# A sparse-graph kernel on one core: a new order of tile visits, a fifth sum bank, and VectorE's half of the split two visits later

## What is computed

```python
for _ in range(3):
    v = mlp(A @ u, uv_W1, uv_b1, uv_W2, uv_b2, uv_W3, uv_b3)
    u = mlp(A @ v, vu_W1, vu_b1, vu_W2, vu_b2, vu_W3, vu_b3)
x = layernorm(x + v)
out = layernorm(x + A @ (x @ weight))
```

## Time and profile before

| | |
|---|---|
| median of three executions | 1225.14 us |
| the profiled execution | 1227.23 us |
| its span, first to last instruction | 1225.5 us |
| mean granted TensorE clock | 0.984 |
| PE busy | 1173.3 us (96%), 5198 matmuls |
| DVE busy | 727.7 us (59%) |
| ACT busy | 666.4 us (54%) |
| HBM read | 262.7 MB, 216 GB/s over the span |
| tile loads | 248 of 1 MB, median 4.9 us from issue to landing |

### The profile page before, as it was taken

How to read it: one execution, slowest core, us unless ns; L and a number is a source line. 1 busy time by engine, 2 the same in 40 slices (tenths; PEclk the granted TensorE clock), 3 DMA queues, 4 the chain that set the end, 5 groups by cost and what they waited for, 6 DMA issues and landing times. The chain is left out here.

```text
span 1225.5 us, 13700 instructions
## 1 busy us (share of the span) xinstructions
PE 1173.3 (96%) x5198; PEld 956.0 (78%) x5198; DVE 727.7 (59%) x857; ACT 666.4 (54%) x837; POOL 10.6 (1%) x24
## 2 busy tenths in 40 slices
PE   5999999999999999999999999999977889999986
PEld 4788888888788888788888788888855778887875
DVE  5976555556555544745454854555653445559886
ACT  5876544446554544654444754445644345566774
POOL 2000000000000000000000000000000000000000
PEclk9999999999999999999999999999988889999999
DMA  9977665655545546744445844465542334558883
GB/s 355 384 287 275 237 231 207 239 206 215 198 172 210 188 162 231 274 162 179 175 187 194 309 173 168 172 240 206 208 171 103 138 138 171 207 206 312 324 312 150
DMA packets 37535, 265.72 MB, mean 217 GB/s; under 512 B 4432, under 2 KB 4432, under 8 KB 5600
## 3 DMA queue, kind: packets, MB, share of 16 engines
q1 hardware_dynamic: 36576, 262.68, 57.5%
q0 software_dynamic: 896, 2.17, 0.5%
HBM read 262.74 MB, written 2.10 MB: 216 GB/s over the span
## 5 line engine op out<-in xcount | busy, mean ns | idle before, releaser
L551 DVE TENSOR_TENSOR low<-raw,high 128x1024 fp32r<-128x1024 f32 x496 | 588.9, 1221 | 361.1 <-ACT high L427 360.9
L771 PE MATMUL acc<-high,p_low 128*128 128x512 f32 x1536 | 623.5, 406 | 40.1 <-DVE p_low L643 19.6
L771 PE MATMUL acc<-low,p_high 128*128 128x512 f32 x1536 | 604.3, 393 | 0.0
L771 PE MATMUL acc<-high,p_high 128*128 128x512 f32 x1536 | 604.0, 393 | 0.0
L427 ACT ACTIVATE high<-raw 128x1024 fp32r<-128x1024 f32 x496 | 494.9, 1049 | 58.6 <-PE acc L771 34.6
L771 PEld LDWEIGHTS acc<-high,p_low 128*128 128x128 f32 x1536 | 292.0, 190 | 113.1 <-DVE low L551 27.1
L771 PEld LDWEIGHTS acc<-high,p_high 128*128 128x128 f32 x1536 | 292.4, 190 | 66.0 <-issue 7.4
L771 PEld LDWEIGHTS acc<-low,p_high 128*128 128x128 f32 x1536 | 291.8, 190 | 62.9
L454 ACT ACTIVATE h_high<-h 128x512 fp32r<-128x512 f32 x16 | 10.1, 632 | 119.5 <-DVE h L585 119.5
L585 DVE TENSOR_TENSOR h<-acc,part 128x512 f32<-128x512 f32 x35 | 24.1, 688 | 74.9 <-PE acc L771 70.4
L479 ACT ACTIVATE p_high<-h 128x512 fp32r<-128x512 f32 x32 | 20.2, 632 | 65.1 <-DVE h L600 65.1
(11 more groups left out here) (64 smaller groups left out, 372.5 us busy)
## 6 DMA issues: line engine op xcount, KB each, us to landing
raw<-adj_dram SPq DMA_DIRECT2D x248, 1024.0 KB, 4.9
out_dram<-part POOLq DMA_DIRECT2D x6, 256.0 KB, 4.5
resid<-x_dram SPq DMA_DIRECT2D x1, 1024.0 KB, 17.6
resid<-x_dram SPq DMA_DIRECT2D x2, 256.0 KB, 5.3
resid<-x_dram SPq DMA_DIRECT2D x1, 512.0 KB, 11.7
out_dram<-part SPq DMA_DIRECT2D x2, 256.0 KB, 2.0
w_uv_W<-uv_W_dram POOLq DMA_DIRECT2D x3, 64.0 KB, 7.8
w_vu_W<-vu_W_dram POOLq DMA_DIRECT2D x3, 64.0 KB, 7.8
```

Of the source, the lines that this page charges most:

```text
L551: nc.vector.tensor_tensor(low[t % SLOTS][:], raw_of(t), high[t % SLOTS][:].bitcast(F32), ALU.subtract).then_inc(low_ready, 1)
L771: done = nc.tensor.matmul(bank[:], p[parity][:, at:at + D], a[slot][:, columns], start=(n == s.opens and j == 0 and m == 0), stop=(n == s. ...
```

## The change

It has five parts.

- `sweep` is rewritten. In products 1 to 3 the visits are the same but two more of them (row 3 with band 0) stand between chunk 0's close and its first use, and the tiles of row 2 and of that piece are kept for their second visit. In product 4 ten visits of filling work stand there instead of six, and the tiles of three bands that would be visited twice are loaded twice instead.
- `SPACING` of product 4 is 2 in place of 4. The steps of product 5 no longer count as `halves` (it has no layers, so no instruction depends on it).
- Five banks for sums, and one for projections in place of two. So a layer 3 waits for the bias add of the chunk just before it, and a projection for the residual add of the chunk just before it.
- `LAG` = 2: DVE's `low` of a tile is placed four visits ahead of its opening visit, no longer six. ACT's `high` stays at six.
- `HELD` = 8 in place of 6.

The number of tiles goes from 496 to 500 (two more loads of 1 MB); visits, chunks and sums stay at 768, 48 and 95.

```diff
-BANKS = 4
-HELD = 6
+
+LAG = 2
+BANKS = 5
+HELD = 8
...
-SPACING = [2] * NORMED + [4, 3]
+SPACING = [2] * LAST + [3]
...
+        def some(r, places, total):
+            return self.one(rows[r], self.band([rows[i] for i in places]), total)
+
+        for r in range(OPENED + 1):
+            opened[r] = self.open(k, rows[r], "finish")
+        for r in [*range(1, OPENED + 1), 0]:
+            some(r, [r], opened[r])
+        some(1, [0], opened[1])
+        if k < NORMED:
+            fill = {4: [4], 5: [5], 6: [6]}
+        else:
+            fill = {5: [5], 6: [6, 5], 7: [7, 6]}
+        for r, places in fill.items():
+            some(r, places, self.open(k, rows[r], "more" if r < CHUNKS - 1 else "keep"))
+        of_2 = some(2, [0, 1], opened[2])
+        of_3 = some(3, [0], opened[3])
+        for r in (1, 2, 3):
+            kept[r] = self.open(k + 1, rows[r], "keep")
+        some(1, [0], kept[1])
+        for t in of_2:
+            self.visit(t, kept[2])
+        for t in of_3:
+            self.visit(t, kept[3])
+        self.both(rows[3], self.band(rows[1:3]), opened[3], kept[3], 0)
+        for r in range(OPENED + 1, CHUNKS):
+            first = self.open(k, rows[r], "finish" if r in fill or r < CHUNKS - 1 else "whole")
+            second = self.open(k + 1, rows[r], "keep")
+            if r not in fill:
+                some(r, [r], first)
+            alone = [i for i in fill.get(r, []) if i != r]
+            shared = [rows[i] for i in range(r) if i not in alone]
+            self.both(rows[r], self.band(shared), first, second, HELD if r == CHUNKS - 1 else 0)
+            some(r, alone, second)
...
-        proj = [psum(f"proj{i}", [D, CHUNK]) for i in range(2)]
+        proj = psum("proj", [D, CHUNK])
...
+        lowered_at = [max(max(split_at[u], plan.opening[u] - AHEAD + LAG) for u in range(t + 1))
+                      for t in range(len(tiles))]
...
-                    if n == split_at[t]:
+                    if n == lowered_at[t]:
                         if t % IN_BAND == 0 and t // IN_BAND < CHUNKS:
                             lower_x(t // IN_BAND)
                         split(t)
...
             def layer_3(i):
                 pe.wait_ge(second_ready, i + 1)
-                if i >= 2:
-                    pe.wait_ge(biased, i - 1)
+                if i:
+                    pe.wait_ge(biased, i)
...
-                if i >= FINAL + 2:
-                    pe.wait_ge(x_added, i - NORM - 1)
+                if i > FINAL:
+                    pe.wait_ge(x_added, i - NORM)
                 else:
-                    pe.wait_ge(biased, i - 1)
+                    pe.wait_ge(biased, FINAL)
```

More of the change, by code:

```diff
@@ L152, in sweep @@
         rows = list(range(CHUNKS)) if k % 2 == 0 else list(range(CHUNKS))[::-1]
[L153 to L174, removed]
@@ L175, in sweep @@
-        self.both(rows[-1], self.band(rows[:-1]), first, self.open(k + 1, rows[-1], "keep"), HELD)
+        opened, kept = {}, {}
+        def some(r, places, total):
[9 more added lines that the diff above has]
+            fill = {5: [5], 6: [6, 5], 7: [7, 6]}
@@ L203, in place_chunks @@
             row = s.chunk if s.product % 2 == 0 else CHUNKS - 1 - s.chunk
-            halves = row not in WHOLE_ROWS or (s.product == 0 and row < CHUNKS - 1)
+            halves = s.product < LAST and (row not in WHOLE_ROWS or (s.product == 0 and row < CHUNKS - 1))
             self.chunks.append(Chunk(i, s.read, s.read + (LAYER_3 if halves else WHOLE_LAYER_3), halves))
@@ L209, in place_parts @@
         for s in self.sums:
-            for before in self.sums:
-                if (before.product, before.chunk, before.goal) == (s.product - 1, s.chunk, "finish") and s.goal == "keep":
+            if s.goal == "keep":
+                read = [b for b in self.sums if b.goal == "finish" and b.closes < s.closes
+                        and b.chunk % (CHUNKS - 1) == s.chunk % (CHUNKS - 1)]
+                if read:
+                    before = max(read, key=lambda b: b.closes)
                     s.read = max(s.read, before.read + 1)
@@ L600, in add_bias @@
                 nc.vector.tensor_tensor(
-                    h[i % 2][:].rearrange("p (j d) -> p j d", d=D), proj[i % 2][:].rearrange("p (j d) -> p j d", d=D),
+                    h[i % 2][:].rearrange("p (j d) -> p j d", d=D), proj[:].rearrange("p (j d) -> p j d", d=D),
                     b_spread[f"{way_of(i)}_b3"][:].unsqueeze(1).to_broadcast([D, IN_CHUNK, D]),
@@ L618, in measure @@
                     dve.wait_ge(proj_done, i + 1)
-                    source = proj[i % 2]
+                    source = proj
                     dve.wait_ge(normed_ready, i - NORM)
@@ L726, in turning @@
                 for j in range(IN_CHUNK):
-                    done = nc.tensor.matmul(block_in(proj[i % 2], j), block_in(source, j), weight[:], start=True,
+                    done = nc.tensor.matmul(block_in(proj, j), block_in(source, j), weight[:], start=True,
                                             stop=True)
```

## The result

| | before | after |
|---|---|---|
| median in the first comparison (4 executions each) | 1224.80 us | 1184.12 us |
| ratio after to before | | 0.967, interval 0.9644 to 0.9695 |
| the profiled execution's span | 1225.5 us | 1182.2 us |
| mean granted clock | 0.984 | 0.999 |

The change takes 40.7 us off (3.3%); forecast were 1186 us and a range from 1178 to 1204. Part 2 of the page, the lines that answer to the earlier trace rows, shows where it came from: the valley in slices 30 to 33 and its lower clock are gone.

The account below looks back on a forecast made before the run. PE bound, losing 33.4 us in product 4's opening and 10.9 in the DVE-bound last sweep. Terms -30.9 - 7.4 - 1.0 = -39.3 took 1227.23 to 1187.9; 2.1 off for the median gave 1186 us, range 1178 to 1204.

Parts of the forecast that it names:

- Parts 1 and 2: Product 4's opening: more visits before p's first use, chain to p_low 13.3 to 8.5 us; all four p_low waits go.
- Rival D: Product 4's opening: p is late for another reason, two or three 5 us waits stay; 1207 us; chance 4%.
- Part 3: Product 4's opening: PE's 2.8 us wait for a sum bank goes, as five banks give every sum three visits.
- Part 4: Product 4's opening, places 583 to 591: DVE's bunched work leaves 2.5 us of the 33.4 lost, so -30.9 us.
- Part 5: Last sweep: without DVE's 13.5 us of waiting for ACT, PE's 10.9 us loss becomes 3.5, so -7.4 us.
- Rival B: Last sweep gives nothing: shorter lead, later raw buffers and one projection bank eat the gain; 1193 us; chance 17%.
- Part 6: Loads: two more in product 4 cost 0 us; in the last sweep bandwidth is barely enough, within the 3.5 us.
- Part 7: Start: DVE reaches the first chunk's lower_sum two splits earlier; PE waits 2.14 us there; -1.0 us, between 0 and -2.5.
- Rival A: Lag does nothing for the chain; chunks 2 and 3 keep 2.5 us waits, last sweep its loss; 1203; chance 8%.
- Rival C: Everywhere: four visits of lead are too few, tiles late by one visit at each chunk; +26 us, 1251; chance 4%.

Follow-up runs that it names:

- e2: The changed kernel's order of visits alone, with LAG = 0, four sum banks and two projection banks: 1207.57 us, ratio 0.9854.
- e1: The kernel before with the lag of 2 alone (old order, four sum banks, two projection banks): 1190.18 us, ratio 0.9707.
- e5: The changed kernel with product 4's filling as in products 1 to 3, six visits instead of ten: 1185.29 us, ratio 0.9674.
- e3: The changed kernel with four sum banks and two projection banks: 1184.28 us, ratio 0.9661.
- e12: The changed kernel with the old sweep, HELD = 6 and old SPACING, keeping LAG = 2, five sum banks and one projection bank: 1188.22 us, ratio 0.9688.
- e9: The changed kernel run again, unaltered: 1184.29 us.
- e6: The changed kernel with LAG = 1 in place of 2: 1182.35 us, ratio 0.9654.
- e8: The changed kernel with last-sweep loads cut to the first of their two tiles (for timing only): 1182.71 us, ratio 0.9645.
- e11: The changed kernel with AHEAD = 7, LAG = 2, four sum banks and two projection banks: 1188.26 us.
- e10: The changed kernel with LAG = 1, four sum banks and two projection banks: 1182.33 us.

## Why the prediction was right, and where it was not

**Parts 1 and 2** were right in mechanism and size. The opening's loss went from 33.4 to 1.5 us against 2.5 forecast; the chain takes 8.1 us against 8.5; e2's waits of 3.3 and 2.5 us against 2.5 and 2.5 show that for chunks 2 and 3 the room alone wasn't enough, and e1 that for chunks 0 and 1 the lag alone is nearly enough (waits of 1.0 and 1.8 us where 3.5 and 5.6 were). What the prediction did not say is how much the two overlap: alone they are worth 35 and 18 us, together 41. And ten visits of filling gain little over six once the chain takes 8 us (e5). Rival D falls with the profile after, which has no wait for `p_low`; but e2 shows what would have come of the order alone, two of the four waits at 3.3 and 2.5 us.

**Part 3** named the right wait and the wrong cure. The sum took 2.8 us for the fifth bank. e3 shows that it is worth nothing in the new order, since the order itself puts two visits between a bank's read and its reopening; and e1 that the lag alone takes 1.9 of the 2.8 us, as the add that frees the bank is DVE's and stood behind one of its waits for ACT. In the old order e12 removes the 0.9 us that is left. What I set against it in the prediction (the Trainium skill, "TensorE: Matmul & The Clock Gate", section "HAM oscillation — how this bites in real kernels": more PSUM buffering gave no further gain) came out better for the bank than my reading of the row: 1184.28 us with four sum banks, 1184.12 with five. The total didn't suffer, as the wait did go. That is luck: another part of the change took it away.

**Part 4** was right that DVE falls a little behind in the bunch: there is one stall, at visit 595 and not 591, of 1.0 us against 2.5. It was not the wait for `low` that I forecast: 0.7 of it is layer 1 waiting for DVE's sum of chunk 2.

**Part 5** was right, 3.5 us left as forecast. That it agrees to the tenth is chance: the same stretch (visit 696 to 767) takes 106.0 us after, 105.4 in the same kernel run again (e9) and 104.6 in e3. DVE's idle time for ACT went from 13.5 to 0.6 us; e1 shows 1.9 with the old order. Rival B falls with it: the shorter lead doesn't eat the gain. But its fear has a place, as lag 4 shows. The lag of 2 was not the best value: with 1 PE doesn't wait for `low` at all from 50 us on, in e6.

**Part 6**: loads cost about 1.4 us (e8, not clear of noise), inside the 3.5. **Part 7**: the start is 2.3 us shorter by visit 568, forecast 1.0; the wait for `lower_sum` fell from 2.14 to 0.98 us and one of 0.28 us for ACT came, and the 3.4 us at the lower clock behind that wait, 47.0 to 50.4 us in the profile before, did not come. PE's first visit starts between 9.3 (e5) and 10.5 us (e6) in the runs, 10.2 before and 9.7 after, so 0.5 of the 2.3 us, and up to a microsecond of any run's start, are chance.

**The total** came out 2 us below the forecast, and two errors of it lean on each other. The parts gave 43.3 us in the profiled executions (2.3 up to visit 568, 32.3 in product 4, 8.7 in the last sweep) where the sum had 39.3, so the profiled execution was 1183.93 us and not 1187.9. The 2.1 us that I took off for the median then didn't come: it is 1184.12.

Rival A falls with e1. Rival C did not come at lag 2: between 50 and 860 us PE waits for nothing. That `HELD` or `SPACING` have a part of their own was not tried by itself. One slip in the description of the change: the tiles of two bands are loaded twice, not of three (rows 6 and 7 of the sweep); this is the four tiles more, 500 for 496.

## What to carry to other kernels

When two engines make two halves of one thing and both also serve a chain that goes to and fro between them, give them different places in their queues. Two places of difference were worth 35 of 41 us here by themselves; with the new order one place did as well as two, while four cost 24 us against two. Before moving work to make room between a result and its use, look at what stands inside the chain: three idle times of 1.3 to 3.3 us were half its length. A wait for a buffer that a row names may go with the order rather than with another buffer; try it alone.

## What the runs showed that I had not expected

A lag of one place does as well as two, even where a tile opens only every second visit. I expected 1186 to 1196 us and measured 1182.35: as far as the profiles show, what matters is that ACT's `high` isn't behind the very step that itself waits for DVE.

Placing ACT's split one visit earlier (e11) cost 6 us against e10, with the same lead for DVE, and 4 us against e3, with the same lag.

ACT waited 15.9 us for loads in the last sweep, twice as long as before (8.4), and halving the loads gave about 1.4 us, not clear of noise: a growing wait on an engine ahead of the bound need not cost much. That it grows because ACT arrives earlier is my reading; no run separates it.
